# Convolution stage: three tap stages summed on VectorE and one on GpSimd in place of three on VectorE, with 512 KB block loads in a ring of six on SyncE's queue

## The chip, the cores and the metric

The kernel runs on one core of a Trainium2 chip. The metric is the device time of one execution in microseconds (us); three executions of the kernel before gave a median of 874.47 us (874.31 to 874.52).

## The reference

The program is one block of a network on `x` of shape (2, 512, 256): `x` plus a block-sparse causal convolution of its layer norm, then a mixture of 16 experts with a shared expert, then attention, then the mixture again. The change touches the convolution alone:

```python
n_blocks, bs, _, ks = block_values.shape          # 128, 64, 64, 16
x_unfold = xb[:, cols].reshape(batch, n_blocks * bs, t)
W = block_values.reshape(n_blocks * bs, bs, ks)
o = jax.lax.conv_general_dilated(x_unfold, W, window_strides=(1,), padding=[(ks - 1, 0)],
    dimension_numbers=('NCH', 'OIH', 'NCH'), feature_group_count=n_blocks)
y = jnp.zeros((batch, n_block_row, bs, t), o.dtype).at[:, rows].add(o)
```

There are 128 weight blocks of 64 x 64 with 16 taps. Blocks with the same (column, row) pair of channel blocks act on the same input and add into the same output, so the kernel first sums the weights of equal pairs (at most 64 pairs) and then convolves once with the sums. With the drawn data columns and rows are below 4, so 16 pairs are live; a flag guards the other 48.

## The kernel before

Two taps make a tap stage (`NST` = 8 stages). The weight blocks of a stage are summed in one of two ways:

- **On TensorE, stages 0 to 4** (`NPE` = 5). `bank_blocks(c)` (L244) has SyncE load a 512 KB chunk of the weights of all 128 blocks; eight chunks make a stage (`SB` = 8), 40 in all. `sum_bank` (L528) multiplies a chunk with a one-hot matrix, which leaves the sums of a "bank" in PSUM. ScalarE copies them out (`round_banks`, L285 and L286), VectorE makes the low part (`low_banks`, L397), and TensorE may sum bank c only once the low part of bank c - 4 is made. Chunks lie in a ring of six buffers, so chunk c is loaded once bank c - 6 is summed.
- **On VectorE, stages 5 to 7** (`ND` = 3). GpSimd's queue loads 16 transfers of 768 KB, eight blocks each with all three stages (L348), into three buffers (`raw_d`, tile `cv_shared`; two of the three lie under the normalized input and wait for `xc_lo_done`). `add_block` (L413) adds a block into `acc` at an offset held in a register: two adds of 128 x 96 elements for a block (L421), each of which waits for the one before. `load_pairs` (L409) brings eight offsets into registers. `BANK_BLOCKS` says how many blocks VectorE adds behind the low part of each bank from stage 2 on.

The products of a stage are 24 matmuls of 512 columns (`products`, L545). `sum_and_convolve` (L604) puts the products of stage st - 1 between the banks of stage st. The products of the last stage summed on TensorE follow behind the last bank (`convolve_last_banks`); the products of stages 5 to 7 can only start once all 128 blocks are added (`convolve_added`, L586: four pieces of a row pair each wait for their low sums, `low_sums`, L405). In `convolve_added` all stages' first row pair comes first (12 matmuls a stage), then the second row pair, with the transposes of the next layer norm (`turn`, L129) ahead of the last 12 matmuls. Behind them follows the first mixture layer.

SyncE, GpSimd and VectorE each run their own instructions in program order, so an instruction that waits holds up all behind it on that engine.

Of the kernel before, what the change touches and what calls it, by code (L numbers as in the profile page):

```python
# [11 lines left out]
F32 = mybir.dt.float32  # L12
# [7 lines left out]
P = 128  # L20
# [10 lines left out]
NPE, ND = 5, 3  # L31
OB, DB, RING = 8, 8, 6
# [129 lines left out]
def conv_phase(nc, cm, pm, ps, ins, following, prefetch, first_weights):  # L162


    with ExitStack() as ctx:
# [3 lines left out]
        DROW = ND * BS  # L169
        NDC = NBLK // DB  # L170
        shared = sb("shared", [P, 3 * DB * DROW], F32)
        raw_d = [shared[:, i * DB * DROW:(i + 1) * DB * DROW].rearrange("p (n f) -> p n f", n=DB) for i in (2, 0, 1)]
# [4 lines left out]
        raw += [sb(f"raw{i}", [P, CHUNK], F32)[:] for i in range(2, RING)]  # L177
# [3 lines left out]
        ws_hi += [sb(f"ws_hi{i}", [P, NLOW, BS], F32R)[:] for i in range(2, ND + 1)]  # L181
        ws_lo += [sb(f"ws_lo{i}", [P, NLOW, BS], F32R)[:] for i in range(2, ND + 1)]
        full = [sb(f"full{i}", [P, NW - NLOW, BS], F32) for i in range(2)]
        acc = sb("acc", [P, ND, NW, BS], F32)
        colrow = sb("colrow", [P, 2], I32)
# [16 lines left out]
            "zeros_ready", "ones_ready", "cr_in", "line_in", "iota_done", "const_done",  # L202
            "cr_conv", "pair_part", "pair_ready", "onehot_ready", "acc_zeroed", "added",
# [5 lines left out]
        raw_d_in = [cm(f"cv_raw_d_in{i}") for i in range(3)]  # L209
# [9 lines left out]
        BANK_BLOCKS = ((5,) * 8, (5,) * 8, (6, 6, 6, 6, 6, 4, 0, 0))  # L219
# [7 lines left out]
        def slot_of(st):  # L227
            return st % 2 if st <= NPE else st - NPE + 1
# [4 lines left out]
        def piece_of(st, r):  # L233
            return NPE * SB + r * ND + (st - NPE)
# [8 lines left out]
        def sync(sp):  # L243
# [21 lines left out]
            for c in range(6, NPE * SB):  # L265
                bank_blocks(c)
            prefetch[0](sp)

        def scalar(a):
# [18 lines left out]
            def round_sums(st, r):  # L288
                e = st - NPE
                a.activation(row_part(ws_hi[slot_of(st)], r), row_part(acc[:, e, 0:NLOW, :], r), ACT.Copy)\  # L290
                 .then_inc(s["ws_hi_done"], 1)

            a.wait_ge(s["ones_ready"], 1)
# [19 lines left out]
        def gpsimd(g):  # L313
            g.iota(pair_iota[:], pattern=[[NW // 2, 2], [NCB // 2, 2], [NCB, NCB // 2], [1, NCB // 2]], base=0,
                   channel_multiplier=0).then_inc(s["iota_done"], 1)
# [6 lines left out]
            g.wait_ge(s["const_done"], 4)  # L322
# [52 lines left out]
        def vector(v):  # L375
            v.memset(zeros[:], 0.0).then_inc(s["zeros_ready"], 1)
            v.memset(ones[:], 1.0).then_inc(s["ones_ready"], 1)
# [3 lines left out]
            v.wait_ge(s["iota_done"], 1)  # L381
# [20 lines left out]
            def low_sums(st, r):  # L402
                e = st - NPE
                v.wait_ge(s["ws_hi_done"], piece_of(st, r) + 1)
                v.tensor_tensor(row_part(ws_lo[slot_of(st)], r), row_part(acc[:, e, 0:NLOW, :], r),  # L405
                                row_part(ws_hi[slot_of(st)].bitcast(F32), r), ALU.subtract).then_inc(s["ws_lo_done"], 1)

            def load_pairs(d):
                return nc.values_load_multi_w_load_instructions(  # L409
                    line_pair[0:1, d * DB:(d + 1) * DB], engines=[mybir.EngineType.DVE], min_val=0, max_val=NW - 1,  # L410
                    skip_runtime_bounds_check_because="columns and rows are numbers of channel blocks, 0 to 7 each")[1]

            def add_block(i, pairs):  # L413
                d, n = divmod(i, DB)
                if n == 0:
                    v.wait_ge(raw_d_in[d % 3], 16 * (d // 3 + 1))
                for k in range(2):
                    part = slice(k * BS // 2, (k + 1) * BS // 2)
                    dst = acc[:, :, bass.ds(pairs[n], 1), part].rearrange("p e a f -> p e (a f)")
                    src = raw_d[d % 3][:, n, :].rearrange("p (e f) -> p e f", e=ND)[:, :, part]  # L420
# [66 lines left out]
            for i in range(2, FIRST_BLOCKS):  # L487
                add_block(i, pairs if i < DB else more)
            done, pairs = FIRST_BLOCKS, more
            for st in range(2, NPE):  # L490
                for q in range(SB):
                    low_banks(st, range(q, q + 1))
                    end = done + BANK_BLOCKS[st - 2][q]
                    edge = -(-done // DB) * DB
                    more = load_pairs(edge // DB) if edge < end else pairs
                    for i in range(done, end):
                        add_block(i, pairs if i < edge else more)
                    done, pairs = end, more
            for r in range(GC // 2):
# [11 lines left out]
        def tensor(t):  # L511


            t.wait_ge(s["zeros_ready"], 1)
# [8 lines left out]
            t.wait_ge(s["ones_ready"], 1)  # L523
# [25 lines left out]
            def high_products(st):  # L549

                for c in range(NCB):
                    for r in range(GC):
                        if c >= NCB // 2 or r >= GC // 2:
# [3 lines left out]
                            else:  # L557
                                sums = acc[:, e, w:w + 2, :]
# [27 lines left out]
            def convolve_added():  # L586
                for st in range(NPE, NST):
                    t.wait_ge(s["ws_lo_done"], piece_of(st, 0) + 1)
                    with t.If(flag != 0):
                        t.wait_ge(s["added"], 2 + 2 * NBLK)  # L590
                        high_products(st)
# [84 lines left out]
def ffn_phase(nc, cm, pm, ps, ins, tag, factors, turn_banks, unfinished, prefetched, following, qkv, first_weights, ended, closing, out):  # L676

    with ExitStack() as ctx:
# [29 lines left out]
            "last_w_in", "last_hi_done", "last_lo_done", "scaled_done", "h_ready", "h_hi_done", "h_lo_done", "down_done", "y_ready", "x_added", "out_done")}  # L708
# [1189 lines left out]
def build(nc, ins, out):  # L1898
    with ExitStack() as ctx:
# [14 lines left out]
            "rstd": sb("rstd", [P, NT], F32),  # L1914
            "first_w": sb("first_w", [P, FIRST_W2 + D], F32),
            "spare": sb("spare", [P, 1], F32),
# [116 lines left out]
```

## Time and profile before

| what | value |
|---|---|
| median of the three runs | 874.47 us |
| span of the profiled execution, first to last instruction | 873.0 us |
| own time of the profiled execution outside its span | not shown apart; the median lies 1.5 us above the span |
| TensorE (PE) busy | 865.5 us, 99% of the span |
| VectorE (DVE) busy | 501.8 us, 57% |
| ScalarE (ACT) busy | 420.0 us, 48% |
| GpSimd (POOL) busy | 320.0 us, 37% |
| convolution | from 0 to 126.3 us |

The page gives shares over the whole span. The convolution is its first seventh, and there the DMA engines and VectorE are loaded in a way that the shares over the span don't show; the prediction reads that stretch by itself.

### The profile page before, as it was taken

The numbers are of one execution on the slowest core, as the hardware profiler recorded it, in microseconds if no ns is written. First come the engines' busy times: TensorE is split into PE (matmuls) and PEld (weight loads), VectorE is DVE, ScalarE is ACT, GpSimd is POOL, SyncE is SP. The second block draws the span as 40 slices with busy tenths as digits, with TensorE's granted clock in tenths as the row PEclk, the third lists the DMA queues.
The fourth block names the chain that finished last, engine by engine and source line by source line (L and its number), as shares of the span: only waits on it lengthen the run. The fifth ranks groups of instructions, "written<-read, shape, count | busy, mean of one in ns | idle before, by whom it ended". The sixth has DMA issues, their size and how long they took to land.

```text
span 873.0 us, 16737 instructions
## 1 busy us (share of the span) xinstructions
PE 865.5 (99%) x5617; PEld 773.3 (89%) x5620; DVE 501.8 (57%) x1360; ACT 420.0 (48%) x978; POOL 320.0 (37%) x293
## 2 busy tenths in 40 slices
PE   9999999999999999999999999999999999999998
PEld 7999878888888888889989998998997888888887
DVE  4777757333333338887688668768877433333334
ACT  3522416334334344776377557647746433434332
POOL 5211014556555564232121213212112556556552
PEclk9999999999999999999999999999999999999999
DMA  8999312111111102000000100000002111111111
GB/s 338 362 383 391 136 40 77 49 54 36 54 45 45 54 18 76 1 26 21 18 3 21 36 0 24 0 0 1 1 1 73 38 54 39 51 54 36 54 36 49
DMA packets 25554, 61.01 MB, mean 70 GB/s; under 512 B 3298, under 2 KB 10916, under 8 KB 25508
## 3 DMA queue, kind: packets, MB, share of 16 engines
q1 hardware_dynamic: 23204, 47.82, 16.1%
q0 software_dynamic: 2304, 12.58, 3.8%
q8 instruction: 28, 0.46, 0.2%
q14 instruction: 18, 0.15, 0.0%
HBM read 59.35 MB, written 1.05 MB: 69 GB/s over the span
## 4 chain that ended last, share of the span: by engine, by line
PE 93%; DVE 3%; ACT 1%; DMA 1%; issue 1%; POOL 0%; DVEq 0%; ACTq 0%
PE bank L1131 29%; PE bank L1655 25%; PE bank L1144 14%; PE bank L534 7%; PE bank L545 5%; PE bank L1781 4%; PE bank L1721 3%; PE bank L1157 2%; PE bank L1167 2%; DMA cv_shared<-in_wtaps 1%; PE bank L1746 1%; DVE cv_acc L421 1%; PE bank L518 1%; PE bank L1675 1%; PE bank L129 0%
## 5 line engine op out<-in xcount | busy, mean ns | idle before, releaser
L1030 DVE TENSOR_TENSOR f_h<-f_scaled,bank 128x512 f32<-128x512 f32 (+1 forms) x90 | 60.8, 676 | 179.4 <-POOL f_scaled L895 166.9
L812 ACT ACTIVATE f_h_hi<-f_h 128x512 fp32r<-128x512 f32 (+2 forms) x102 | 63.6, 624 | 186.2 <-DVE f_h L1030 186.0
L895 POOL TENSOR_TENSOR f_scaled<-f_act,f_gate_rows 128x512 f32<-128x512 f32 x80 | 102.9, 1287 | 116.3 <-ACT f_act L805 115.9
L1131 PE MATMUL bank<-f_xt_hi,f_w_lo 128*128 128x512 f32 x352 | 138.2, 393 | 0.0
L1131 PE MATMUL bank<-f_xt_hi,f_w_hi 128*128 128x512 f32 x352 | 137.8, 391 | 0.0
L1350 ACT ACTIVATE at_prob<-bank,at_sbias,at_qrs 128x512 f32<-128x512 f32 (+3 forms) x128 | 77.6, 618 | 72.6 <-DVE at_sbias L1542 72.6
L1037 DVE TENSOR_TENSOR f_h_lo<-f_h,f_h_hi 128x512 fp32r<-128x512 f32 (+2 forms) x102 | 71.8, 704 | 70.7 <-ACT f_h_hi L812 70.4
L1131 PE MATMUL bank<-f_xt_lo,f_w_hi 128*128 128x512 f32 x352 | 108.8, 390 | 0.0
L1144 PE MATMUL bank<-f_w_lo,f_h_hi 128*128 128x256 f32 (+1 forms) x352 | 99.6, 283 | 0.0
L1144 PE MATMUL bank<-f_w_hi,f_h_lo 128*128 128x256 f32 (+1 forms) x352 | 99.6, 283 | 0.0
L1144 PE MATMUL bank<-f_w_hi,f_h_hi 128*128 128x256 f32 (+1 forms) x352 | 99.3, 282 | 0.0
L805 ACT ACTIVATE f_act<-bank 128x512 f32<-128x512 f32 (+2 forms) x102 | 59.9, 589 | 52.6 <-PE bank L1131 46.4
L1413 POOL TENSOR_TENSOR at_qrs<-at_qsum,minus_half 128x4 f32<-128x4 f32 x32 | 32.8, 1025 | 137.7 <-DVE at_qsum L1503 137.7
L1131 PEld LDWEIGHTS bank<-f_xt_lo,f_w_hi 128*128 128x128 f32 x352 | 66.1, 188 | 14.4
L1131 PEld LDWEIGHTS bank<-f_xt_hi,f_w_lo 128*128 128x128 f32 x352 | 66.4, 189 | 11.1
L1131 PEld LDWEIGHTS bank<-f_xt_hi,f_w_hi 128*128 128x128 f32 x352 | 66.5, 189 | 11.0
L1144 PEld LDWEIGHTS bank<-f_w_hi,f_h_lo 128*128 128x128 f32 (+1 forms) x352 | 67.2, 191 | 3.4
L1144 PEld LDWEIGHTS bank<-f_w_hi,f_h_hi 128*128 128x128 f32 (+1 forms) x352 | 67.2, 191 | 3.3
L884 POOL TENSOR_TENSOR f_w_lo<-f_wraw,f_w_hi 128x512 fp32r<-128x512 f32 x46 | 59.5, 1293 | 25.3 <-ACT f_w_hi L791 25.3
L1144 PEld LDWEIGHTS bank<-f_w_lo,f_h_hi 128*128 128x128 f32 (+1 forms) x352 | 67.2, 191 | 0.0
L1538 DVE TENSOR_REDUCE at_smax<-bank 128x1 f32<-128x512 f32 (+3 forms) x128 | 58.8, 485 | 2.3 <-PE bank L1655 2.0
L889 POOL TENSOR_TENSOR f_w_lo<-f_wraw,f_w_hi 128x256 fp32r<-128x256 f32 x46 | 43.9, 954 | 35.1 <-ACT f_w_hi L797 35.1
(232 smaller groups left out, 2062.8 us busy)
## 6 DMA issues: line engine op xcount, KB each, us to landing
cv_raw<-in_wconv SPq DMA_DIRECT2D x26, 512.0 KB, 6.7
cv_shared<-in_wtaps POOLq DMA_DIRECT2D x16, 768.0 KB, 7.7
f_wraw<-in_w SPq DMA_DIRECT2D x42, 256.0 KB, 2.6
xn<-in_wconv SPq DMA_DIRECT2D x14, 512.0 KB, 6.5
f_wraw<-in_w SPq DMA_DIRECT2D x42, 128.0 KB, 2.5
at_wraw<-in_wqkv SPq DMA_DIRECT2D x3, 768.0 KB, 4.4
at_oraw<-in_wo SPq DMA_DIRECT2D x4, 512.0 KB, 3.5
X<-in_x_tiles SPq DMA_DIRECT2D x2, 512.0 KB, 8.0
```

Source lines behind the costliest of these rows:

```text
L534: m = t.matmul(ps[q % BANKS][:].rearrange("p (w o) -> p w o", o=OB)[:, :, o], raw[c % RING][:, o * P:(o + 1) * P], onehot[:], start=True, ...
L805: a.activation(act[half][0:rows, cols], pg[half][0:rows, cols], ACT.Silu).then_inc(s["act_done"], 1)
L812: a.activation(h_hi[slot][0:rows, cols], h_f[half][0:rows, cols], ACT.Copy).then_inc(s["h_hi_done"], 1)
L884: g.tensor_tensor(w_lo[slot][:, 0:n], raw_views(m, slot, rows)[0], w_hi[slot][:, 0:n].bitcast(F32), ALU.subtract).then_inc(s["w13_lo_done" ...
L895: g.tensor_tensor(scaled[half][:], act[half][:], gate_rows[:, half * HALF:(half + 1) * HALF], ALU.mult).then_inc(s["scaled_done"], 1)
L1030: v.tensor_tensor(h_f[half][0:rows, cols], src[half][0:rows, cols], pu[half][0:rows, cols], ALU.mult)\
L1037: v.tensor_tensor(h_lo[slot][0:rows, cols], h_f[half][0:rows, cols], h_hi[slot][0:rows, cols].bitcast(F32), ALU.subtract).then_inc(s["h_lo ...
L1131: mm = t.matmul((pg, pu)[gu][half][0:out_rows, :], w, x, start=q == 0, stop=q == 3 * KH - 1)
L1144: mm = t.matmul(bank, h[hslot][0:rows, tok], w, start=first and q == 0 and j % 2 == 0, stop=False, skip_group_check=True)
L1350: a.activation(prob[:, sl, POFF[j]:POFF[j + 1]], ps[bank][:, col:col + n], ACT.Exp, bias=sbias[:, sl, j:j + 1], scale=qrs[:, sl, j:j + 1], ...
L1538: v.tensor_reduce(smax[:, sl, j:j + 1], ps[bank][:, col:col + P * (j + 1)], AX_X, ALU.max)\
L1655: m = t.matmul(dst, l, r, start=start and q == 0, stop=stop and q == 2, skip_group_check=in_opened_bank)
```

## The change

Stage 4 is no longer summed on TensorE: `NPE` is 4, so 32 chunks of 512 KB are left. Stages 4 to 7 are summed from the blocks (`NADD` = 4): 4, 5 and 6 on VectorE with the same two adds of 128 x 96 for a block, stage 7 on GpSimd with one add of 128 x 64 for a block into a tile of its own (`acc_g`), each waiting for the one before. The block loads are 32 transfers of 512 KB (four blocks with four stages each) in a ring of six buffers, so 24 blocks may be in flight, as before. They are issued by SyncE, in one written order with the chunks (`tap_blocks` and the loop behind it), where `blocks_behind` places them. A transfer with d of 6 or more waits for `added` of VectorE and `added_g` of GpSimd. `BANK_BLOCKS` is six blocks behind each bank of stages 2 and 3, and the last 18 blocks follow behind the last bank. The second `full` buffer lies over the buffers for the rounded sums of the added stages, and ScalarE waits for the products of stage 3 (`ws_free`) before it rounds the sums of the added stages. The sixth chunk buffer lies in `first_w`, so that tile's load waits for all 32 banks.

```diff
-NPE, ND = 5, 3
-OB, DB, RING = 8, 8, 6
+NPE, ND, NG = 4, 3, 1
+NADD = ND + NG
+OB, DB, PB, RING, DRING = 8, 4, 8, 6, 6
...
-        BANK_BLOCKS = ((5,) * 8, (5,) * 8, (6, 6, 6, 6, 6, 4, 0, 0))
+        BANK_BLOCKS = ((6,) * 8, (6,) * 8)
...
+        def blocks_behind(c):
+
+            if c < 2 * SB - 1:
+                return 0
+            between = [n for blocks in BANK_BLOCKS for n in blocks]
+            return NBLK if c >= NPE * SB else FIRST_BLOCKS + sum(between[:c - 2 * SB + 1])
...
+            def tap_blocks(d):
+                if d >= DRING:
+                    sp.wait_ge(s["added"], 2 + 2 * DB * (d - DRING + 1))
+                    sp.wait_ge(s["added_g"], 1 + DB * (d - DRING + 1))
+                elif d >= DRING - B:
+                    sp.wait_ge(s["xc_lo_done"], 4 * (d - DRING + B + 1))
+                sp.dma_start(raw_d[d % DRING], ins["wtaps"][d].rearrange("p (n f) -> p n f", n=DB))\
+                  .then_inc(raw_d_in[d % DRING], 16)
...
-            for c in range(6, NPE * SB):
-                bank_blocks(c)
+
+            d = 0
+            for c in range(RING, NPE * SB + 2 * RING):
+                if c < NPE * SB:
+                    bank_blocks(c)
+                while d < NDC and (c >= 2 * d + RING + 2 if d < DRING - B else c >= SB + 4 * (d - DRING + B) + 11 if d < DRING else
+                                   blocks_behind(c - RING - 1) >= DB * (d - DRING + 1)):
+                    tap_blocks(d)
+                    d += 1
+            sp.wait_ge(s["summed"], NPE * SB)
             prefetch[0](sp)
...
-            a.wait_ge(s["ws_free"], NPE + 1)
+            a.wait_ge(s["ws_free"], NPE + 2)
             a.wait_ge(s["added"], 2 + 2 * NBLK)
             for r in range(GC // 2):
                 for st in range(NPE, NST):
+                    if st == NST - 1 and r == 0:
+                        a.wait_ge(s["added_g"], 1 + NBLK)
                     round_sums(st, r)
...
-            for d in range(NDC):
-                if d in (1, 2):
-                    g.wait_ge(s["xc_lo_done"], 4 * d)
-                if d >= 3:
-                    g.wait_ge(s["added"], 2 + 2 * DB * (d - 2))
-                g.dma_start(raw_d[d % 3], ins["wtaps"][d].rearrange("p (n f) -> p n f", n=DB)).then_inc(raw_d_in[d % 3], 16)
+            def add_last_stage(p):
...
+                for i in range(p * PB, (p + 1) * PB):
+                    d, n = divmod(i, DB)
+                    if n == 0:
+                        g.wait_ge(raw_d_in[d % DRING], 16 * (d // DRING + 1))
+                    dst = acc_g[:, bass.ds(pairs[i % PB], 1), :].rearrange("p a f -> p (a f)")
+                    add = g.tensor_tensor(dst, dst, raw_d[d % DRING][:, n, ND * BS:], ALU.add)
+                    add._wait_ge(s["added_g"], i + 1)
+                    add.then_inc(s["added_g"], 1)
+
+            g.memset(acc_g[:], 0.0).then_inc(s["added_g"], 1)
+            g.wait_ge(s["cr_conv"], 8)
+            for p in range(NBLK // PB):
+                add_last_stage(p)
```

On SyncE's queue the chunks from chunk 18 on (counted from 0) stood like this before; `xn` and `cv_raw` are chunk buffers (L247). The pattern goes on to chunk 39, and behind it stands the load of `first_w`.

```order
L247 DMA xn<-in_wconv 128x1024 [waits cv_summed] x2
L247 DMA cv_raw<-in_wconv 128x1024 [waits cv_summed] x4
L247 DMA xn<-in_wconv 128x1024 [waits cv_summed] x2
L247 DMA cv_raw<-in_wconv 128x1024 [waits cv_summed] x4
L247 DMA xn<-in_wconv 128x1024 [waits cv_summed] x2
```

In the changed kernel the same queue holds, from chunk 18 on (L265 are chunks, L280 the block transfers into `cv_shared`, `cv_raw_first` is the sixth chunk buffer):

```order
L265 DMA xn<-in_wconv 128x1024 [waits cv_summed] x2
L280 DMA cv_shared<-in_wtaps 128x1024 [waits cv_xc_lo_done]
L265 DMA cv_raw<-in_wconv 128x1024 [waits cv_summed] x3
L265 DMA cv_raw_first<-in_wconv 128x1024 [waits cv_summed]
L280 DMA cv_shared<-in_wtaps 128x1024 [waits cv_xc_lo_done]
L280 DMA cv_shared<-in_wtaps 128x1024 [waits cv_added_g,cv_added] x5
L265 DMA xn<-in_wconv 128x1024 [waits cv_summed]
L280 DMA cv_shared<-in_wtaps 128x1024 [waits cv_added_g,cv_added]
L265 DMA xn<-in_wconv 128x1024 [waits cv_summed]
L280 DMA cv_shared<-in_wtaps 128x1024 [waits cv_added_g,cv_added] x2
L265 DMA cv_raw<-in_wconv 128x1024 [waits cv_summed]
L280 DMA cv_shared<-in_wtaps 128x1024 [waits cv_added_g,cv_added]
```

The fifth block transfer stands behind chunk 19, the sixth to the eleventh behind chunk 23, and from the seventh on each waits for the adds of both engines, with the following chunks queued behind that wait.

On GpSimd's engine the block transfers stood between the clearing of the sums and the first weights' low part (L157):

```order
L331 MEMSET cv_acc 128x3x1024 [waits cv_flag_ready]
L331 MEMSET cv_acc 128x3x1024 x2
L338 TENSOR_TENSOR cv_rstd<-cv_var_eps,minus_half 128x4 [waits cv_var_ready] x2
L331 MEMSET cv_acc 128x3x1024 [waits cv_xn_ready]
L348 DMA cv_shared<-in_wtaps 128x1536 [waits cv_rstd_ready]
L348 DMA cv_shared<-in_wtaps 128x1536 [waits cv_xc_lo_done] x2
L348 DMA cv_shared<-in_wtaps 128x1536 [waits cv_added] x13
L157 TENSOR_TENSOR first_lo<-first_w,first_hi 128x416 [waits f1_w13_hi_done]
```

In their place stand the clearing of `acc_g`, a load of eight offsets, and for each block a register instruction and an add of 64 elements (this pattern goes on to block 128):

```order
L368 MEMSET cv_acc 128x3x1024 [waits cv_xn_ready]
L393 MEMSET cv_acc_g 128x4096 [waits cv_rstd_ready]
L381 TENSOR_LOAD cv_line_pair [waits cv_cr_conv]
L389 ISA [waits cv_raw_d_in0]
L389 TENSOR_TENSOR cv_acc_g<-cv_acc_g,cv_shared 128x64 [waits cv_added_g]
L389 ISA
L389 TENSOR_TENSOR cv_acc_g<-cv_acc_g,cv_shared 128x64 [waits cv_added_g]
```

All transfers are gone from GpSimd's engine, and 128 adds, each waiting for the one before, and 16 offset loads have come; the work of the mixture layer on GpSimd stands behind them.

## Rows read from the trace of the kernel before

**Rows 1.** The page: head and busy time of each engine.
```profile
span 873.0 us, 16737 instructions
...
PE 865.5 (99%) x5617; PEld 773.3 (89%) x5620; DVE 501.8 (57%) x1360; ACT 420.0 (48%) x978; POOL 320.0 (37%) x293
```

**Rows 2.** The chain that ended last, first 200 us: start, duration, what.
```profile
1.20 4.54 PE bank L518 x11
...
5.86 1.19 PE bank L518 x5
7.06 25.22 PE bank L534 x224
...
101.65 0.41 DVE held L397 x2
...
102.10 5.87 PE bank L545 x24
...
107.98 2.95 PE bank L545 x12
...
122.57 0.87 PE bank L129 x8
123.44 2.88 PE bank L545 x24
```

**Rows 3.** Busy time by stretch: the engines, PEclk, DMA share, GB/s.
```profile
0.00:7.06 7.06, 5.84 (x19) 1.96 (x19) 1.23 (x9) 1.49 (x2) 3.17 (x15) 1.00 0.59 211
...
45.00:95.00 50.00, 50.00 (x384) 46.93 (x384) 38.83 (x215) 13.18 (x40) 6.45 (x12) 1.00 0.99 384
95.00:102.10 7.10, 6.63 (x48) 5.82 (x47) 6.46 (x36) 2.34 (x7) 0.00 (x0) 1.00 0.04 15
```

**Rows 4.** SyncE's queue in order of time.
```profile
35.52 10.03 SPq L247 DMA_DIRECT2D cv_raw<-in_wconv  x4
47.01 3.52 SPq L247 DMA_DIRECT2D xn<-in_wconv  x2
```

**Rows 5.** VectorE in order of time: adds, low parts of banks, low sums.
```profile
38.77 4.14 DVE L421 TENSOR_TENSOR cv_acc<-cv_acc,cv_shared 128x96 f32 x24 [0.36 <-issue]
...
44.96 1.78 DVE L421 TENSOR_TENSOR cv_acc<-cv_acc,cv_shared 128x96 f32 x10 [0.47 <-issue]
46.65 0.28 DVE L397 TENSOR_TENSOR held<-bank,held 128x128 fp32r<-128x128 f32 x1
46.85 1.76 DVE L421 TENSOR_TENSOR cv_acc<-cv_acc,cv_shared 128x96 f32 x10
...
49.08 1.61 DVE L421 TENSOR_TENSOR cv_acc<-cv_acc,cv_shared 128x96 f32 x9 [0.26 <-issue]
...
102.40 0.69 DVE L405 TENSOR_TENSOR held<-cv_acc,held 128x512 fp32r<-128x512 f32 x1 [0.36 <-ACT held L290]
```

**Rows 6.** GpSimd in order of time: the last clearing of sums.
```profile
21.67 2.66 POOL L331 MEMSET cv_acc<- 128x3072 f32 x1 [1.48 <-DVE cv_shared L441]
```

**Rows 7.** GpSimd's groups, shapes apart, whole span: busy, mean ns | idle before.
```profile
L907 POOL TENSOR_TENSOR f_scaled<-f_act,f_gate_rows 128x256 f32<-128x256 f32 x4 | 2.9, 736 | 6.5 <-ACT f_act L805 6.5
...
L667 POOL TENSOR_TENSOR held<-f_qkv_raw,held 128x512 fp32r<-128x512 f32 x1 | 1.3, 1281 | 0.0
```

**Rows 8.** GpSimd, then VectorE, in order of time, 326 to 331 us.
```profile
327.07 2.41 POOL L671 TENSOR_TENSOR held<-f_qkv_raw,held 128x1024 fp32r<-128x1024 f32 x1
329.43 1.75 POOL L907 TENSOR_TENSOR f_scaled<-f_act,f_gate_rows 128x512 f32<-128x512 f32 x1
...
327.15 0.69 DVE L1030 TENSOR_TENSOR f_h<-f_scaled,bank 128x512 f32<-128x512 f32 x1 [1.39 <-POOL f_scaled L907]
328.54 1.50 DVE L1037 TENSOR_TENSOR f_h_lo<-f_h,f_h_hi 128x512 fp32r<-128x512 f32 x1 [0.70 <-ACT f_h_hi L812]
```

**Rows 9.** Line L1037 on VectorE: duration ns min/median/max.
```profile
L1037 DVE TENSOR_TENSOR f_h_lo<-f_h,f_h_hi x102: 418/693/1497, 133.1 to 868.1; 128x512 fp32r<-128x512 f32 x94, 96x512 fp32r<-96x512 f32 x4, 128x256 fp32r<-128x256 f32 x4
```

More of the change, by code:

```diff
@@ L176, in conv_phase @@
         raw = [following_xn[:, i * CHUNK:(i + 1) * CHUNK] for i in range(2)]
-        raw += [sb(f"raw{i}", [P, CHUNK], F32)[:] for i in range(2, RING)]
+        raw += [sb(f"raw{i}", [P, CHUNK], F32)[:] for i in range(2, RING - 1)]
+        raw += [nc.alloc_sbuf_tensor_at("cv_raw_first", [P, CHUNK], F32, offset=pm["first_base"])[:]]
         NLOW = NW // 4
@@ L180, in conv_phase @@
                          .rearrange("p (w o) -> p w o", w=NLOW) for i in range(2)] for part in range(2))
-        ws_hi += [sb(f"ws_hi{i}", [P, NLOW, BS], F32R)[:] for i in range(2, ND + 1)]
-        ws_lo += [sb(f"ws_lo{i}", [P, NLOW, BS], F32R)[:] for i in range(2, ND + 1)]
-        full = [sb(f"full{i}", [P, NW - NLOW, BS], F32) for i in range(2)]
+        shared_base = nc.sbuf_base
+        ws_hi += [sb(f"ws_hi{i}", [P, NLOW, BS], F32R)[:] for i in range(2, NADD)]
+        ws_lo += [sb(f"ws_lo{i}", [P, NLOW, BS], F32R)[:] for i in range(2, NADD)]
+        full = [sb("full0", [P, NW - NLOW, BS], F32),
+                nc.alloc_sbuf_tensor_at("cv_full1", [P, NW - NLOW, BS], F32, offset=shared_base)]
         acc = sb("acc", [P, ND, NW, BS], F32)
+        acc_g = sb("acc_g", [P, NW, BS], F32)
         colrow = sb("colrow", [P, 2], I32)
@@ L208, in conv_phase @@
         x_in = [cm(f"cv_x_in{b}") for b in range(B)]
-        raw_d_in = [cm(f"cv_raw_d_in{i}") for i in range(3)]
+        raw_d_in = [cm(f"cv_raw_d_in{i}") for i in range(DRING)]
         X = pm["X"]
@@ L342, in gpsimd @@
             g.wait_ge(s["rstd_ready"], B)
-            for d in range(NDC):
-                if d in (1, 2):
-                    g.wait_ge(s["xc_lo_done"], 4 * d)
-                if d >= 3:
-                    g.wait_ge(s["added"], 2 + 2 * DB * (d - 2))
-                g.dma_start(raw_d[d % 3], ins["wtaps"][d].rearrange("p (n f) -> p n f", n=DB)).then_inc(raw_d_in[d % 3], 16)
+            def add_last_stage(p):
+                pairs = nc.values_load_multi_w_load_instructions(
+                    line_pair[0:1, p * PB:(p + 1) * PB], engines=[mybir.EngineType.Pool], min_val=0, max_val=NW - 1,
+                    skip_runtime_bounds_check_because="columns and rows are numbers of channel blocks, 0 to 7 each")[1]
+                for i in range(p * PB, (p + 1) * PB):
[10 more added lines that the diff above has]
+                add_last_stage(p)
             first_weights["low"](g)
@@ L487, in vector @@
             for i in range(2, FIRST_BLOCKS):
-                add_block(i, pairs if i < DB else more)
+                add_block(i, pairs if i < PB else more)
             done, pairs = FIRST_BLOCKS, more
@@ L493, in vector @@
                     end = done + BANK_BLOCKS[st - 2][q]
-                    edge = -(-done // DB) * DB
-                    more = load_pairs(edge // DB) if edge < end else pairs
+                    edge = -(-done // PB) * PB
+                    more = load_pairs(edge // PB) if edge < end else pairs
                     for i in range(done, end):
@@ L498, in vector @@
                     done, pairs = end, more
+            while done < NBLK:
+                edge = -(-done // PB) * PB
+                if done == edge:
+                    pairs, edge = load_pairs(done // PB), done + PB
+                for i in range(done, edge):
+                    add_block(i, pairs)
+                done = edge
             for r in range(GC // 2):
@@ L557, in high_products @@
                             else:
-                                sums = acc[:, e, w:w + 2, :]
+                                sums = added_sums(e)[:, w:w + 2, :]
                             for x in (xc_hi, xc_lo):
```

53 lines of the change are left out of this document (29 added, 24 removed).

## The prediction

> **What bounds the kernel now.** I read the page first: TensorE is busy for 99% of the span [rows 1], so a microsecond comes off the kernel only where TensorE's own work ends sooner. The chain of waits then shows that within the convolution it runs through TensorE from 7 us on, apart from a detour through the block adds before 102 us [rows 2]. The reader is to see two things there. The last bank's products run from 102.10 to 107.97, while the adds of the blocks were complete at 101.65: the adds had about 5 us of cover. And from 107.98 the products of the added stages run to 126.32 (72 matmuls and the transposes, 18.34 us), with nothing waited for. The view by stretch shows what else is full there: from 45 to 95 us the DMA engines are busy for 99% at 384 GB/s, and VectorE for 38.8 of 50 us; behind 95 us DMA is empty [rows 3]. So three engines run level up to about 100 us, and a gain on TensorE alone moves the end only if the other two follow.
>
> **What the change removes.** Eight banks go. Fourteen banks took 25.22 us [rows 2], 1.80 us each, so TensorE sheds 8 x 1.80 = 14.4 us. The products stay 24 matmuls a stage, 5.87 us [rows 2], but those of stage 4 now stand behind the complete adds instead of beside them.
>
> **What sets the end.** Let D be the time at which VectorE has added the last block. Between D and the first low sum lay 102.40 + 0.69 - 101.65 = 1.44 us [rows 2, 5]. Behind it follow four added stages, 18.34 + 5.87 us. The convolution ends at D + 1.44 + 24.21 = D + 25.65, against 126.32 before: the kernel gets faster only if D comes before 100.7, a microsecond earlier than the 101.65 of now. TensorE is ready in time: the last 24 banks and three stages' products before 102.10 took 24 x 1.80 + 17.6 = 60.8 us, so they began at 41.3, and now 16 banks and three stages' products follow there: 41.3 + 28.8 + 17.6 = 87.7, if nothing holds it. All turns on D.
>
> **D by the transfers.** The bytes are the same: 40 x 512 + 16 x 768 KB before, 32 x 512 + 32 x 512 KB now. What changes is the order. The sixth block transfer stands behind chunk 23, and the four chunks 20 to 23 are issued until 35.52 + 10.03 = 45.55 [rows 4]; their times stay, since TensorE's banks up to 18 stay. A transfer of 0.524 MB takes 1.37 us at 384 GB/s, so with the chunk ahead of it the sixth lands at about 49. VectorE has by then added the 20 blocks of the first five transfers and stands still from about 46.7. From chunk 22 on, at 43.4, 37 transfers are left: 37 x 1.37 = 50.6 us, that is 94.0, with about 1.3 us for the last to land 95.3. Four blocks behind it give D = 96.7, the earliest possible.
>
> **D by VectorE's own work.** Twenty-four adds in 4.14 us are (4.14 - 0.25) / 23 = 0.169 us from start to start [rows 5] (0.25 is one add's own duration, 1.78 less nine steps), 0.338 us a block. A low part between two runs of adds costs 0.19 us (the run ends at 46.74, the next starts at 46.85 and would have started 0.08 before the end), with an offset load 0.55 (48.61 to 49.08) [rows 5]. Behind 49.0 there are 108 blocks, 15 low parts and 14 offset loads: 36.5 + 2.9 + 5.0 = 44.4, so 93.4. Alone VectorE would be done before the transfers, and D stays 96.7.
>
> **The adds on GpSimd.** No row shows an add of 64 elements. Two-input operations took 736 ns at 256 elements and 1281 ns at 512 [rows 7], 2.13 ns an element and 192 ns fixed, so an add of 64 is 0.33 us, of which 0.136 us is reading. With register work and a sixteenth of an offset load for each I take 0.40 us a block; the lower bound is 0.33, and the upper is open (0.7 would be one fixed part of 192 ns twice more). They start at 21.67 + 2.66 [rows 6] plus 3.5 us for clearing `acc_g`, about 28, so up to 49 us GpSimd too does its 20 blocks, for nothing. Then 108 x 0.40 = 43 us: 92, hidden, if that were all.
>
> **What the two adds do to each other.** This is the cost that decides. At 328.54 VectorE starts an operation with two SBUF inputs while GpSimd reads through a long one of its own (327.07 to 329.48). It takes 1.50 us where the median is 0.693, and ends at 330.04, 0.56 us behind GpSimd's end: it stood still until GpSimd was through. GpSimd's next one, started at 329.43, takes 1.75 and ends 1.14 us behind VectorE's, its 512 elements of reading: now it had stood [rows 8, 9]. At 327.15 an operation of VectorE with one input in PSUM took 0.69 beside the same GpSimd operation, unharmed [rows 8]. So two-input operations of the two engines run one at a time, and every add of both engines here has two SBUF inputs. The Trainium skill (SBUF — State Buffer, "Who interferes with whom") states it as an exclusive lock on a read interface the two engines share, held for the whole instruction; the trace agrees, and by that rule the two streams can't overlap, while by VectorE's and GpSimd's rows taken alone D would stay at 96.7.
>
> The price of one GpSimd add to VectorE: at most its reading and a hand-over, 0.136 + 0.02 = 0.156 us; at least that less the 0.07 us for which VectorE is between two reads anyway (0.169 less 96 elements at the 1.04 ns an element that the 0.533 of 512 implies), 0.086 us; and nothing, if so short an add slips through. A block then takes 0.494 or 0.424 us. The 7.9 us of low parts and loads leave room for about 20 GpSimd adds for nothing. D = 49.0 + 53.4 + 7.9 - 3.1 = 107.2 at the upper price, 49.0 + 45.8 + 7.9 - 1.7 = 101.0 at the lower. I take the middle, 104.1, since neither row shows operations as short as these: the convolution ends 104.1 + 25.65 - 126.32 = 3.4 us later.
>
> **TensorE's clock.** TensorE now stands idle ahead of the added products. The low part of bank 31 comes 24 blocks and three loads before D, 24 x 0.46 + 1.1 = 12.1 us, so at 92; the last bank's products end at about 98, and the next start at 105.5, 7.5 us later. Before there was no such pause (6.63 of 7.10 us busy from 95 on [rows 3]). The only matmuls that follow idle time are the kernel's first: 11 of 512 columns in 4.54 us, 0.413 each, the pace of 1.2 GHz, then 5 in 1.19, 0.238 each, that of 2.4 GHz, although the column shows a granted clock of 1.00 for the stretch [rows 2, 3]. The same again would cost 4.54 - 11 x 0.238 = 1.9 us. The bounds are 0 and 1.9; I take 1.9, since the pause is longer than the 1.20 us ahead of the first matmul. The Trainium skill (TensorE: Matmul & The Clock Gate, "What you observe") has the same slow start; no row shows a pause in mid-kernel.
>
> **At no cost:** the transfers' issue on SyncE (0.45 us each, while it waits for most of the time); the later load of `first_w`, which has from about 98 us to the first layer's start at 126; clearing `acc_g`, hidden as GpSimd has nothing else; two more pieces of rounding and low sums, 0.69 us each against 12 matmuls of 2.95 [rows 2, 5]. If GpSimd were late its stage comes third behind the others, with 3 x 2.95 = 8.9 us of cover.
>
> **Sum.** 3.4 + 1.9 = 5.3 us slower. The profiled execution has a span of 873.0, with the median of the runs 1.5 above it; the sum is made in that execution and added to the median: 874.5 + 5.3 = 879.8.
>
> **The rivals.**
> - *The short adds hardly disturb each other, and the transfers bound D.* For it: an add reads for 0.1 us and might fit between; DMA is full up to 95. Against it: rows 8. D = 96.7 is 4.0 us sooner: 870.5, or 872.4 with the slow clock. It decides from a price of an add below 0.08 us. 28%.
> - *The middle ground*, D near 100 to 102 with or without the clock, within 1.75 us of before (0.2%, about what a measurement of this kernel can tell from no change): 12%.
> - *GpSimd is late.* If a block takes it 0.6 us (a slow dependent add), it ends at 49 + 65 = 114, and its stage starts at 115.2 instead of 114.4 or sooner; behind that start come 2.95 + 8.85 + 0.87 + 2.88 = 15.6 us: 130.8, 4.5 us later, 6.4 with the clock: 880.9. It decides from 0.52 us a block; at 0.7 it is 15 us. It also holds the ring, and SyncE's queue with it. 12%.
> - *The forecast:* adds that hinder each other, 48%, with its own range of 876.5 to 884.5.
>
> **The numbers.** The slower cases hold 60%, faster 28%, same 12%. The range goes from the first rival's time without the clock, 870.5, to the upper price with the clock (107.2: 6.5 + 1.9, 882.9) and half of the late GpSimd's excess beyond: 886.
>
> **What would show it.** Right: VectorE's adds (0.251 us each before) with a mean near 0.3, GpSimd's at 0.35 to 0.45, the last add at 101 to 107, a TensorE pause of over 5 us, then products of 0.43 us a step for some 4 us. Wrong: adds unchanged at 0.25 and a last add at 97, with VectorE waiting for `cv_shared` transfers; or GpSimd's adds at 0.6 and more, with ScalarE waiting for `cv_acc_g`; or TensorE at full pace behind the pause; or the sixth transfer landing long before 49.

## The result, and the profile after

The changed kernel takes 881.82 us (median of 4 runs, 881.70 to 882.55), the kernel before 874.39 us on the same chip (874.24 to 874.52): a ratio of 1.0086, 95% interval 1.0072 to 1.0101, that is 7.5 us slower. 879.8 was predicted, with a range of 870.5 to 886.0 and a chance of 60% for slower.

The chain that ended last, first 200 us (start, duration, what; "..." stands for pieces left out):

```profile
7.40 25.22 PE bank L589 x224
...
45.93 5.44 DMA cv_shared<-in_wtaps
...
58.39 0.35 DVE cv_acc L469 x2
...
58.85 0.35 DVE cv_acc L469 x2
...
103.99 1.77 DVE cv_acc L469 x10
...
105.85 0.64 ACT held L325
...
106.51 0.70 DVE held L453
107.21 0.50 issue
107.72 10.53 PE bank L600 x36
...
118.29 11.30 PE bank L600 x48
129.59 0.87 PE bank L130 x8
130.47 2.88 PE bank L600 x24
```

Against [rows 2] the reader is to see three things. The chain leaves TensorE at 45.5 us for the sixth block transfer and comes back to it only at 107.7; in between it runs through VectorE's adds, a block (two adds) every 0.46 us. The last add ends at D = 105.76 instead of 101.65, 4.1 us later. And from there to the end of the convolution it is 133.35 - 105.76 = 27.6 us; before it was 126.32 - 101.65 = 24.7, with another stage's products to fill the time behind D. The convolution ends 133.35 - 126.32 = 7.03 us later, and the spans differ by 880.0 - 873.0 = 7.0: nothing behind the convolution changed.

The two engines that add, grouped by line with shapes apart, first 140 us (busy, mean ns | idle time before and what ended it), then line L389 by itself (ns min/median/max):

```profile
L469 DVE TENSOR_TENSOR cv_acc<-cv_acc,cv_shared 128x96 f32 x256 | 56.6, 292 | 7.9 <-DMA cv_shared<-in_wtaps 3.9 <-issue 2.1 <-DVE cv_acc L469 0.7
L389 POOL TENSOR_TENSOR cv_acc_g<-cv_acc_g,cv_shared 128x64 f32 x128 | 53.2, 416 | 22.6 <-DMA cv_shared<-in_wtaps 9.4 <-POOL cv_acc_g L389 4.5
...
L389 POOL TENSOR_TENSOR cv_acc_g<-cv_acc_g,cv_shared x128: 317/383/2995, 28.2 to 103.6; 128x64 f32 x128
```

VectorE, then TensorE's two long waits, in order of time (compare [rows 5]; before, TensorE had no such waits):

```profile
45.30 2.11 DVE L469 TENSOR_TENSOR cv_acc<-cv_acc,cv_shared 128x96 f32 x12 [0.47 <-issue]
47.33 0.28 DVE L445 TENSOR_TENSOR held<-bank,held 128x128 fp32r<-128x128 f32 x1
51.50 2.77 DVE L469 TENSOR_TENSOR cv_acc<-cv_acc,cv_shared 128x96 f32 x12 [3.89 <-DMA cv_shared<-in_wtaps]
...
94.33 1.22 PE L600 MATMUL bank<-cv_xc_hi,held 128*128 128x512 f32 x2 [7.27 <-DVE held L445]
...
107.72 1.22 PE L600 MATMUL bank<-cv_xc_hi,held 128*128 128x512 f32 x2 [5.77 <-DVE held L453]
```

Busy time by stretch (PE | clock granted | DMA share and GB/s in the two wide ones, with all engines as in [rows 3]):

```profile
45.00:95.00 50.00, 41.36 (x281) 38.01 (x281) 44.24 (x198) 9.88 (x30) 33.34 (x90) 0.90 0.98 376
...
92.00:98.00 6.00, 3.67 (x9) 0.50 0.81 285
98.00:102.00 4.00, 3.95 (x18) 0.98 0.06 20
102.00:106.00 4.00, 0.00 (x0) 0.88 0.01 2
106.00:110.00 4.00, 2.28 (x5) 0.50 0.02 4
110.00:114.00 4.00, 4.00 (x15) 0.77 0.01 4
```

From 45 to 95 us VectorE is busy for 44.2 of 50 us where it was 38.8, and TensorE for 41.4 where it was 50.0. The clock drops to 0.50, that is 1.2 GHz, behind each of TensorE's two long waits (7.27 and 5.77 us).

### The profile page after: what moved, and what is told of

Read it like the earlier page. It is cut to its first block, busy times and chain, and to the rows that moved or that the text cites. A ratio compares the mean times of both kernels' runs of the same rounds, so it can differ in the third digit from the quotient of the medians.

```text
span 880.0 us, 16757 instructions
## 1 busy us (share of the span) xinstructions
PE 858.6 (98%) x5488; PEld 765.3 (87%) x5491; DVE 511.9 (58%) x1354; ACT 415.7 (47%) x964; POOL 368.0 (42%) x406
## 4 chain that ended last, share of the span: by engine, by line
PE 88%; DVE 7%; issue 2%; ACT 1%; DMA 1%; DVEq 1%; POOL 0%; SPq 0%; ACTq 0%
PE bank L1187 29%; PE bank L1711 24%; PE bank L1200 14%; DVE cv_acc L469 4%; PE bank L1837 4%; PE bank L589 4%; PE bank L600 3%; PE bank L1777 3%; PE bank L1213 2%; PE bank L1223 2%; PE bank L1802 1%; PE bank L573 1%; DMA cv_shared<-in_wtaps 1%; PE bank L1731 1%; ACT at_prob L1406 0%
## 5 line engine op out<-in xcount | busy, mean ns | idle before, releaser
L1187 PEld LDWEIGHTS bank<-f_xt_lo,f_w_hi 128*128 128x128 f32 x352 | 66.1, 188 | 14.4
L389 POOL TENSOR_TENSOR cv_acc_g<-cv_acc_g,cv_shared 128x64 f32 x128 | 53.2, 416 | 22.6 <-DMA cv_shared<-in_wtaps 9.4
L469 DVE TENSOR_TENSOR cv_acc<-cv_acc,cv_shared 128x96 f32 x256 | 56.6, 292 | 7.9 <-DMA cv_shared<-in_wtaps 3.9
```

The source lines that it names most:

```text
L389: add = g.tensor_tensor(dst, dst, raw_d[d % DRING][:, n, ND * BS:], ALU.add)
L469: add = v.tensor_tensor(dst, dst, src, ALU.add)
L1187: mm = t.matmul((pg, pu)[gu][half][0:out_rows, :], w, x, start=q == 0, stop=q == 3 * KH - 1)
```

## The experiments

Ratios are to the kernel before on the same chip, with their 95% intervals; 0.1% is 0.87 us. In each execution the first bank starts between 6.4 and 7.7 us, by how many of the first 11 matmuls run at half clock, so times of day in a profile are good to some half a microsecond between kernels, and durations and ratios are the firmer evidence.

**e1: no adds on GpSimd.** The adds of stage 7, their offset loads and waits are left out (that stage's sums stay zero); everything else, its products too, stays.

```diff
...
-            for p in range(NBLK // PB):
-                add_last_stage(p)
...
```

> The changed kernel without GpSimd's 128 adds, their offset loads and all waits for them; the sums of stage 7 stay zero, all transfers and all other work stay. Theory (adds of the two engines that both read two SBUF operands run one at a time): a block costs VectorE 0.338 us again in place of the 0.465 of the changed kernel, the sixth block transfer still lands at 51.4, so the last add comes at 96 to 97.5 in place of 105.75 and the time is 872.5 to 874. Rival (the order of the transfers on SyncE's queue and the standstill behind the sixth alone make the loss): the last add stays at 103 to 106 and the time at 879 to 882.

876.99 us, ratio 1.0037 (1.0025 to 1.0050): 4.3 us of the 7.5 are gone. The step came out as the theory said, the last add and the time as neither it nor the rival did. VectorE in order of time:

```profile
51.30 2.12 DVE L448 TENSOR_TENSOR cv_acc<-cv_acc,cv_shared 128x96 f32 x12 [4.06 <-DMA cv_shared<-in_wtaps]
...
76.23 0.76 DVE L448 TENSOR_TENSOR cv_acc<-cv_acc,cv_shared 128x96 f32 x4 [1.07 <-DMA cv_shared<-in_wtaps]
...
86.69 2.12 DVE L448 TENSOR_TENSOR cv_acc<-cv_acc,cv_shared 128x96 f32 x12 [0.26 <-issue]
```

Twelve adds take 2.12 us (median of the runs of twelve) where they took 2.77 in the changed kernel: (2.12 - 0.25) / 11 = 0.170 from start to start, the pace of [rows 5], against 0.229. But the last add ends at 101.05, not at 96.7: VectorE waits for transfers 9.3 us in all, in 8 places up to 83 us, and from 83.8 on, with 42 blocks left, it has no such wait. So neither the transfers' end nor VectorE alone sets D here: transfers that come late in the middle have a part in it.

**e2 and e3: what of a GpSimd add disturbs.** In e2 each add is a memset of 256 elements of `acc_g` (0.311 us where the shortest of the adds took 0.317, but it reads nothing); in e3 it adds 32 of the 64 elements. Stage 7's sums are zero in e2 and half complete in e3. The line taken out is the same in both; e2's line stands first, e3's behind the dots.

```diff
-                    add = g.tensor_tensor(dst, dst, raw_d[d % DRING][:, n, ND * BS:], ALU.add)
+                    add = g.memset(acc_g[:, 4 * (i % 16):4 * (i % 16) + 4, :], 0.0)
...
+                    add = g.tensor_tensor(dst[:, 0:BS // 2], dst[:, 0:BS // 2],
+                                          raw_d[d % DRING][:, n, ND * BS:ND * BS + BS // 2], ALU.add)
```

> The changed kernel with each of GpSimd's 128 adds replaced by a clearing of 256 elements of the same tile, with the same waits, increments and offset loads; it writes, about 0.33 us each, and reads nothing; stage 7 is left zero. Theory (it is GpSimd's reading that holds VectorE up): VectorE's adds are back at 0.169 us from start to start, last add at 96 to 98, time 872.5 to 875. Rival (anything that GpSimd does beside VectorE, its writes, semaphores or offset loads, slows VectorE): last add at 103 to 106, time 879 to 882.

> The changed kernel with GpSimd adding 32 of the 64 elements of each block (half of stage 7 is left out). Theory (VectorE loses GpSimd's reading time): the loss of 0.127 us a block falls by 32 x 2.13 ns = 0.068 to about 0.06, the last add comes at about 98.5 and the time is 874 to 875.5. Rival (a fixed price for each GpSimd instruction): a block stays at 0.465 us for VectorE and the time at 881 to 882.

e2 took 878.37 us, 1.0044 (1.0028 to 1.0061); e3 878.80 us, 1.0060 (1.0043 to 1.0077). Typical runs of twelve adds of VectorE in e2, then in e3:

```profile
88.12 2.12 DVE L469 TENSOR_TENSOR cv_acc<-cv_acc,cv_shared 128x96 f32 x12 [0.26 <-issue]
...
77.15 2.38 DVE L470 TENSOR_TENSOR cv_acc<-cv_acc,cv_shared 128x96 f32 x12
```

128 GpSimd operations of 0.311 us each that only write cost VectorE's adds nothing (2.12 as in e1). With adds of 32 elements the median is 2.38, (2.38 - 0.25) / 11 = 0.194 a step. So a block of VectorE's loses 2 x 0.024 = 0.05 us to a GpSimd add of 32 elements and 2 x (0.229 - 0.170) = 0.12 us to one of 64, somewhat more than in proportion. What hinders is an operation that reads its two inputs; writing alone doesn't. A GpSimd operation with one input was not tried.

The times don't show these prices. The last add comes at 102.46 in e2 and in e3 too, though their steps differ, and at 101.05 in e1; both forecasts of the last add and of the time were missed (too early and too fast). In all three VectorE waits for transfers between 64 and 85 us, 5.2 us in e1, 6.1 in e2 and 1.9 in e3: what e3's adds take longer comes off these waits. e2 and e3 also keep the ring's waits for GpSimd (`added_g`), which e1 drops. e2 is so the closer answer to the question of what the kernel would take if the adds didn't hinder each other: 1.0044, that is 3.7 us of the 7.5 gone; the intervals of e1, e2 and e3 overlap.

**e4: the sixth transfer earlier.** It stands behind chunk 20 instead of 23.

```diff
-                while d < NDC and (c >= 2 * d + RING + 2 if d < DRING - B else c >= SB + 4 * (d - DRING + B) + 11 if d < DRING else
+                while d < NDC and (c >= 2 * d + RING + 2 if d < DRING - B else c >= SB + (d - DRING + B) + 11 if d < DRING else
```

> The changed kernel with the sixth block transfer issued behind chunk 20 in place of chunk 23 (the later ones follow by the same rule, so that the seventh to ninth stand behind chunk 22). Theory: VectorE's and GpSimd's standstill at 47 to 51.5 goes, the last add comes about 3 us sooner, at 102.5 to 103.5, and the time is 878 to 879.5. Rival (the standstill is made up later, since transfers or banks hold VectorE up elsewhere): time 881 to 882.

878.96 us, 1.0060 (1.0043 to 1.0077): 2.3 us less than the changed kernel, as the theory said. The standstill of VectorE at 47.6 us is gone:

```profile
45.29 2.37 DVE L469 TENSOR_TENSOR cv_acc<-cv_acc,cv_shared 128x96 f32 x12 [0.47 <-issue]
...
48.13 2.62 DVE L469 TENSOR_TENSOR cv_acc<-cv_acc,cv_shared 128x96 f32 x12 [0.28 <-issue]
...
67.66 0.89 DVE L469 TENSOR_TENSOR cv_acc<-cv_acc,cv_shared 128x96 f32 x4 [0.59 <-DMA cv_shared<-in_wtaps]
```

VectorE meets four short waits for transfers from 65 us on instead; of the 3.9 us of standstill D gives back 2.7 (103.1).

**e5: TensorE's pause filled.** Twenty-six products of zeros between the last bank's products and the added ones.

```diff
             convolve_last_banks()
+            keep_busy(t, pm, ps[0], 26)
             convolve_added()
```

> The changed kernel with 26 matmuls of zeros (512 columns, into a bank whose sums are spent) between the products of stage 3 and those of stage 4, where TensorE stood idle for 5.8 us; at 0.215 to 0.24 us each they take 5.6 to 6.2 us. Theory (the clock granted at half level behind the pause costs time): the granted clock stays at 1.00 behind the pause and the time falls by 1.5 to 1.9 us, to 880 to 880.3. Rival (the first products are slow for another reason, or the fill delays the added products as much as it saves): time 881.5 to 882.5.

881.40 us, 1.0087 (1.0074 to 1.0101): by the medians 0.4 us less than the changed kernel, by the ratios nothing; the theory had said 1.5 to 1.9. The stretch view and the chain show why:

```profile
98.00:102.00 4.00, 3.92 (x19) 1.00 0.07 24
102.00:106.00 4.00, 3.85 (x18) 1.00 0.01 2
106.00:110.00 4.00, 1.96 (x8) 1.00 0.02 4
...
107.53 1.20 DVE cv_ws_lo L453 x2
108.74 1.21 DVE held L453 x2
109.94 1.22 DVE cv_ws_lo L453 x2
...
111.20 6.09 PE bank L600 x24
```

The clock is 1.00 all through, but the chain now runs through six further low sums to 111.2: products at full pace catch up with VectorE and wait for it. From the first product to the end it is 132.98 - 108.04 = 24.94 us against 25.63: the clock is worth 0.7 us here, of which a D 0.35 us later in this execution (106.10) takes back half.

**e6 to e8: the fourth stage on VectorE.** Both adds of a block are 128 x 128 and GpSimd has none; nothing of the result is left out. e7 adds e4's placing and 20 zero products, e8 e4's placing and more blocks behind the banks, with no zeros. The first edit below is that of all three, the second is e8's.

```diff
-                    src = raw_d[d % DRING][:, n, :].rearrange("p (e f) -> p e f", e=NADD)[:, 0:ND, part]
+                    src = raw_d[d % DRING][:, n, :].rearrange("p (e f) -> p e f", e=NADD)[:, :, part]
...
-        BANK_BLOCKS = ((6,) * 8, (6,) * 8)
+        BANK_BLOCKS = ((6, 7) * 4, (6, 7) * 4)
```

> The changed kernel with all four added stages summed on VectorE: two adds of 128 x 128 for a block in place of 128 x 96, none on GpSimd. Theory (32 more elements cost VectorE 0.033 us an add, less than GpSimd's adds cost it): a block takes 0.404 us in place of 0.465, the last add comes at 103 to 104, and the time is 879 to 880. Rival (GpSimd takes real load off VectorE): time above 882.

> Four stages on VectorE, the sixth transfer behind chunk 20, and 20 matmuls of zeros in TensorE's pause. If the three terms add up (2 to 2.5 us for the adds, 2.9 for the transfer, 1.5 to 1.9 for the clock) the time is 874.5 to 875.5, level with the kernel before. Rival (the terms overlap, since VectorE and the transfers then bound the stretch together): 876 to 878.

> Four stages on VectorE, the sixth transfer behind chunk 20, and 6 and 7 blocks in turn behind each bank in place of 6 and 6 (no filling). The block transfers then stand earlier among the chunks, and TensorE's last products end nearer to the last add, so its pause is about 3 us. Theory (the blocks come late since the chunks go first while TensorE has slack): last add 1 to 2 us sooner than without it and a shorter stretch at half clock, 874 to 875.5. Rival (VectorE's own work bounds it): 876 to 877.

e6 took 879.62 us, 1.0065 (1.0053 to 1.0077); e7 876.99, 1.0036 (1.0023 to 1.0049); e8 876.50, 1.0029 (1.0017 to 1.0041). So e6 came out as its theory said, with the last add at 104.06; e7 and e8 came out as their rivals said: the three terms don't add up. A typical run of VectorE in e6:

```profile
87.56 2.52 DVE L448 TENSOR_TENSOR cv_acc<-cv_acc,cv_shared 128x128 f32 x12 [0.20 <-issue]
```

(2.52 - 0.28) / 11 = 0.204 a step (0.28 is one add's own duration at 128 elements): the fourth stage costs VectorE 0.07 us a block if it does it itself, and 0.12 us if GpSimd does it beside it.

**e9 and e10: the old split behind the new queue.** Five stages on TensorE, three on VectorE, block transfers of 768 KB in a ring of three, but through SyncE's written order; in e9 with the third transfer behind chunk 23, in e10 behind chunk 20 (e4's edit).

```diff
-NPE, ND, NG = 4, 3, 1
+NPE, ND, NG = 5, 3, 0
...
-OB, DB, PB, RING, DRING = 8, 4, 8, 6, 6
+OB, DB, PB, RING, DRING = 8, 8, 8, 6, 3
```

> The old split (five stages summed on TensorE, three on VectorE, none on GpSimd, transfers of 768 KB in three buffers) with the block transfers on SyncE's queue in the written order of the changed kernel. Theory (the queue alone costs nothing as long as the adds are covered): the third transfer, behind chunk 23, makes VectorE stand for 2 to 3 us at 47, the last add comes at 102 to 104, and the last bank's products end at 108 as before, so the time is 874 to 874.8. Rival (the order on one queue is itself a loss): the chunks or the adds come so late that the time is 876 or more.

> As the run with the old split on SyncE's queue, with the third transfer behind chunk 20 in place of chunk 23. Theory: VectorE no longer stands at 47, the last add comes at 100 to 102, and the time stays at 873.8 to 874.5 since the adds had cover anyway. Rival (the queue's order costs elsewhere): the time stays where the other run has it, above 875.

e9 took 882.91 us, 1.0101 (1.0085 to 1.0116); e10 876.91, 1.0036 (1.0022 to 1.0050). Both theories missed, and the rival's 876 or more held for e9. The place of the third transfer, three chunks earlier, is worth 5.7 us in the old split. In e10 the queue doesn't delay the adds: D is 100.7, a microsecond before that of the kernel before. What remains in e10, 3.1 us by the ratio and 2.0 in the span of its profiled execution, is in that execution a wait of ScalarE:

```profile
107.70 0.63 ACT L323 ACTIVATE held<-cv_acc 128x512 fp32r<-128x512 f32 x1 [7.93 <-PE bank L602]
...
109.56 3.10 PE bank L579 x12
```

The rounding of the added sums waits for the products of the last stage summed on TensorE (`ws_free`), since e9 and e10 keep the changed kernel's layout, in which the second `full` lies over the buffers for the rounded sums. In the kernel before the rounding ran at 101.74, beside those products; now the first added product starts at 109.56 instead of 107.98 [rows 2], and the convolution ends 1.9 us later. In the changed kernel this wait was no cost: those products ended at 101.95, before D.

The profiled execution of e9 was its slowest (890.7 us, the other four 881.7 to 883.5), so its times aren't read as e9's. It shows something else, further below.

**e11 and e12: the transfers earlier still, then the pause filled.** e11 is e8 with each block transfer from the seventh on one chunk earlier in the order; e12 is e11 with 16 zero products in the pause.

```diff
-                                   blocks_behind(c - RING - 1) >= DB * (d - DRING + 1)):
+                                   blocks_behind(c - RING) >= DB * (d - DRING + 1)):
```

> Four stages on VectorE, the sixth transfer behind chunk 20, 6 and 7 blocks behind each bank, and each block transfer from the seventh on one chunk earlier in the order. Theory (VectorE's own adds and offset loads, 108 blocks at 0.40 us and about 8 us, bound the stretch, with only 1.4 us of waiting for transfers left): the last add comes at 99.5 to 100.8 and the time is 875.3 to 876.5. Rival (the order still holds it up): 874.5 or less, the kernel level with the one before.

> The kernel of e11_vector_paced_ahead (874.98 us, four added stages on VectorE, low sum last at 99.6 us) with one thing more: 16 products of zeros stand in TensorE's program between the last bank and the added products, where that run has a pause of 3.8 us (97.7 to 101.6 us); after the pause its first 36 products took 10.22 us. Theory that the half clock after the pause costs what the slow products take beyond full speed: the zeros hold the clock at 1.00, the 36 products take about 9.2 us, and the time falls by 0.7 to 1.1 us to 873.9 to 874.3, level with the kernel before. Rival, from e5_pause_filled, where the fill moved the time by less than 0.5 us: the first products wait for their sums instead of running at half clock, and the time stays at 874.7 to 875.2.

e11 took 874.98 us (11 runs), 1.0013 (1.0004 to 1.0022); e12 874.40 us (11 runs), 1.0003 (0.9994 to 1.0012): level with the kernel before. e11's last add came at 99.61, as its theory said, and its time between those of theory and rival. The chain in e11, then in e12:

```profile
101.58 10.22 PE bank L579 x36
...
99.55 3.40 PE bank L60 x15
102.94 8.38 PE bank L579 x36
```

The fill takes the 36 products from 10.22 to 8.38 us. By the medians 0.6 us less came out of it (theory 0.7 to 1.1, rival nothing), but the intervals of e11 and e12 overlap, so that a gain isn't shown. In the profiled execution the zeros ended 1.4 us after e11's first product. They had begun only at 99.55, as the last bank's products, behind a wait of 3.78 us, took 8.35 us, where e11's took 5.9 behind one of 2.16. Fewer zeros weren't tried. No version beat the kernel before.

## Why the prediction was right, step by step

**VectorE's adds decide: right.** From the changed kernel D falls by 4.7 us in e1, 2.7 in e4 and 1.7 in e6, and the median time by 4.8, 2.9 and 2.2.

**Price of a GpSimd add: right within its bounds.** 0.086 to 0.156 us was given, with nothing as a rival. The chain gives 0.46 us a block, less 0.34 in e1: 0.12 us, the middle that was taken. Over the whole stretch from 51.50 to D VectorE took 54.3 us, where 44.4 were reckoned for its own work: the 108 adds of GpSimd cost it 9.9 us, 10.7 were forecast. e2 bears out the mechanism: GpSimd's adds hinder, its writes don't. The Trainium skill (SBUF — State Buffer, "Who interferes with whom") states that a VectorE instruction with two SBUF inputs contends with a GpSimd instruction that reads SBUF, and not with one that only writes it; e2 and e3 agree (0.00 and 0.05 us a block). The size for short adds is from the runs. The prediction's sentence that operations of the two engines "run one at a time" is more than the runs show: see the last section for stretches in which GpSimd's add waited and VectorE lost nothing. The rival "hardly disturb" set its bound at 0.08 us; adds of 32 elements (0.05 us a block in e3) lie below it.

**The sixth transfer lands at 49: mis-sized, 51.4.** The prediction took the DMA engines as full from 43.4 us on. They weren't: SyncE waited before chunk 22 (issued at 43.77) and before chunk 23 (at 45.56), the transfers behind them in the written order waited with it, and the stream ran dry:

```profile
43.00:46.00 3.00, 1.32 (x8) 1.00 0.42 127
46.00:48.00 2.00, 1.61 (x10) 1.00 0.82 227
48.00:51.40 3.40, 0.00 (x0) 1.00 1.02 394
```

The DMA share is 0.42 and then 0.82, which loses 3 x 0.58 + 2 x 0.18 = 2.1 us of a full stream (e11's, with the earlier places, is 0.92 and 0.97; before, with the block transfers on a queue of their own, it was 0.96 and 0.85). The six transfers were then issued within 3.7 us (45.93 to 49.61) and shared the rate, so the sixth took 5.44 us to land. From 51.50 to D it is 54.3 us, where the prediction had 104.1 - 49.0 = 55.1. So D's excess of 1.65 us is this term, in part balanced by the rest.

**Transfers alone would allow D = 96.7: wrong.** e1 took VectorE's hindrance away, and D was 101.05. The prediction reckoned the last transfer's landing and VectorE's work each for itself, both from 49. In fact each bank's chunk stands ahead of its blocks, transfers came late up to 83 us, and what VectorE lost there it couldn't make up behind them: 49.75 us from 51.30 to D, of which 5.2 are waits for transfers, leaving the 44.5 that were reckoned for its own work. So the rival of 28% had the wrong time: had the adds not hindered each other, e1 says 1.0037 x 874.5 = 877.7 and e2, with GpSimd still in the ring's waits, 878.3: slower too, and "faster" deserved less than its 28%.

**D to the first product, 1.44: mis-sized, 1.96.** The missing 0.50 us stands in the chain as TensorE's own issue behind the wait ("107.21 0.50 issue"); before, TensorE was busy until 107.96 with the last bank's products, and no such piece stands in its chain.

**Products and clock, 24.21 + 1.9 = 26.1: 25.63 measured.** The pause of 5.8 us (7.5 predicted, over 5 asked for) was followed by products of 0.43 us for 4 us, as foretold; 36 took 10.53 us, where e12 shows 8.38 at full clock. But at full clock the first products wait for low sums, so the clock's own share is 0.7 us (e5), not 1.9: the sum of 24.21 lacked the low sums' pace, and by e5's 24.94 was 0.7 too low. The two errors partly cancel, so that the 26.1 came out close to the 25.63 in part by luck. Not named was the first pause, 7.27 us at 87 to 94, ahead of the last bank's products; it was covered, as D was later.

**GpSimd late: no.** Its last add ended at 103.95, 1.8 us before D, at 0.44 us an add.

**Sum.** 5.3 predicted; D +1.65 and the rest +0.05 make 7.0 of span, and 7.5 in the runs. Undone singly, GpSimd's adds give back 4.3 us and the sixth transfer's place 2.3; both at once, in e8 with the fourth stage on VectorE and more blocks behind the banks, 5.0; 1.4 more came from the other block transfers' place (e11), and 0.6 to 0.9 from the fill (e12: medians, ratios), which is within the intervals. The change took 14.4 us of banks off TensorE, and none of it came out of any version, since with four stages' products behind D the last add and not TensorE's banks sets the end.

The text ahead of the result said that each of VectorE's adds waits for the one before. More exactly it waits for the one before that (the two halves of a block alternate); GpSimd's wait for the one immediately before.

What stays open: where the time goes in e9's usual executions, as its profile is of another one, what decides at a single add which of the two engines waits, and whether a GpSimd operation with one SBUF input hinders too.

## What to carry to other kernels

Before work is moved to an idle engine, look at whether both engines would read two SBUF operands at a time: here the helper's add cost the bound engine 0.12 us, and doing the same add itself cost it 0.07. In a queue with a written order the place of a single waiting transfer can be worth microseconds (2.3 here, 5.7 in the old split); look at the DMA share by stretch for holes, not at its mean. And when stages are moved from an engine that sums and multiplies in turn to one that must be done before the products start, the whole of their products comes to stand behind that moment.

## What the runs showed of the hardware

- A GpSimd operation that only writes (memset, 0.311 us) didn't slow VectorE's two-input adds (2.12 us for twelve, as with none); an add of 64 elements cost them 0.12 us, one of 32 elements 0.05.
- The hindrance can also fall on GpSimd alone. In the changed kernel its add at 40.51 took 3.00 us (the median of all is 0.383), while VectorE's adds started every 0.169 us, the pace that they have with no GpSimd add beside them (the rows below: VectorE's 20 adds, GpSimd's four). It ended at 43.51, 0.18 us behind the last of VectorE's 20; e2's memset at the same place took 0.311. In e4 it came again: two adds of GpSimd took 1.47 and 2.15 us from 61.28 on, beside 24 adds of VectorE in two runs of 2.11 us.

```profile
39.87 3.46 DVE L469 TENSOR_TENSOR cv_acc<-cv_acc,cv_shared 128x96 f32 x20
...
40.51 4.19 POOL L389 TENSOR_TENSOR cv_acc_g<-cv_acc_g,cv_shared 128x64 f32 x4 [2.24 <-DMA cv_shared<-in_wtaps]
```

- TensorE's half clock followed short waits too. In the changed kernel it followed a wait of 1.23 us (first row; the clock was 1.00 up to it and 0.50 from 70.1 to 72.8). In e9's slowest execution it followed one of 0.57 us, and with TensorE busy all the time the clock stayed at 0.50 for 14 us (26 to 40). The length of the wait alone doesn't decide: in e5 a wait of 3.36 us (second row) was followed by products at full pace, with a granted clock of 1.00 from 92 to 102 us.

```profile
67.08 3.30 PE L589 MATMUL bank<-cv_onehot,cv_raw 128*128 128x64 f32 x16 [1.23 <-DVE held L445]
...
94.31 0.74 PE L600 MATMUL bank<-cv_xc_hi,held 128*128 128x512 f32 x2 [3.36 <-DVE held L445]
...
23.23 6.08 PE L568 MATMUL bank<-cv_onehot,cv_raw 128*128 128x64 f32 x32 [0.57 <-DMA cv_raw<-in_wconv]
...
26.00:30.00 4.00, 4.00 (x21) 4.00 (x20) 1.51 (x2) 2.30 (x5) 0.24 (x1) 0.50 0.77 303
30.00:40.00 10.00, 10.00 (x48) 10.00 (x48) 4.44 (x6) 4.91 (x10) 0.00 (x0) 0.50 0.44 158
```

The last three rows are of that execution of e9, which was 7 to 9 us longer than the others. What else had to come together for it no run shows.
